# Top-k attention on one Trainium2 core: the mask by GpSimd arithmetic instead of GpSimd comparisons and a ScalarE Relu

## What is computed

```python
def attention(x):
    q, k, v = split(x @ Wqkv.T + bqkv)                 # 16 heads of 8
    q, k = layernorm(q), layernorm(k)                  # over the 8 of a head
    aw = softmax(q @ k.T / sqrt(8))                    # 256 x 256 per head
    kth = top_k(aw, 12)[..., -1:]                      # topk = int(256 * 0.05)
    aws = aw * (aw >= kth)
    o_s = (aws / (aws.sum(-1) + 1e-8)) @ v
    qf, kf = softmax(q, -1), softmax(k, -1)
    o_l = qf @ (kf.T @ v) / (qf @ kf.sum(tokens) + 1e-6)
    return (sigmoid(alpha) * o_s + (1 - sigmoid(alpha)) * o_l) @ Wproj.T + bproj

xn = layernorm(x)
y = x + attention(xn) + (xn @ W[idx] + b[idx])         # idx: one of 8, from logits and u
```

## Time and profile before

| what | value |
|---|---|
| median of 3 runs | 1330.32 us |
| lowest and highest | 1327.15 and 1330.66 us |
| span of the profiled execution | 1331.1 us, 0.8 above the median |
| instructions | 40,027 |
| mean granted TensorE clock | 0.930 of full speed |
| busy: PE, DVE, ACT, POOL | 1040.0, 1260.1, 1138.5, 1110.9 us |
| DMA, mean over the span | 62 GB/s, 82.3 MB |

### The profile page before, as it was taken

The page is one execution under the profiler, slowest core; times in us unless marked ns, Lnnn a source line. Parts: engine busy times, 40 slices in busy tenths (PEclk is TensorE's granted clock), DMA queues, the critical chain, the costliest instruction groups (busy, mean ns, idle before and its releaser), DMA issues.

```text
span 1331.1 us, 40027 instructions
## 1 busy us (share of the span) xinstructions
PE 1040.0 (78%) x8964; PEld 693.5 (52%) x8964; DVE 1260.1 (95%) x4916; ACT 1138.5 (86%) x3978; POOL 1110.9 (83%) x1458
## 2 busy tenths in 40 slices
PE   3787877778787878877888787777877788787776
PEld 1455555555455555555555455554555555555544
DVE  5799999999999999999999999999999999999995
ACT  3689998989899888989989899888989888898885
POOL 4588898979789888888879889798888888889874
PEclk9989999989899798998989989898998998989998
DMA  2222222112222122221112221112221212221210
GB/s 57 72 59 63 77 77 75 35 57 64 77 76 72 29 64 65 76 77 47 53 53 76 77 76 46 55 57 71 76 76 35 66 53 76 77 76 33 64 49 13
DMA packets 165131, 82.31 MB, mean 62 GB/s; under 512 B 7747, under 2 KB 164933, under 8 KB 164934
## 3 DMA queue, kind: packets, MB, share of 16 engines
q1 hardware_dynamic: 164934, 80.54, 20.9%
HBM read 42.77 MB, written 37.75 MB: 60 GB/s over the span
## 4 chain that ended last, share of the span: by engine, by line
DVE 57%; issue 33%; DVEq 6%; ACT 1%; POOL 1%; PE 1%; DMA 0%; SPq 0%; POOLq 0%
DVE rest L525 21%; DVE top L518 21%; DVE next L531 8%; DVEq L72 5%; DVE drop L615 2%; DVE o_sparse L574 1%; ACT e L719 1%; DVE den L566 1%; DVE k_sum L593 1%; DVE stats L582 0%; PE work_ps L910 0%; PE work_ps L911 0%; DVE x_mv L588 0%; DVE d_max L557 0%; DVE den L571 0%
## 5 line engine op out<-in xcount | busy, mean ns | idle before, releaser
L386 POOL TENSOR_SCALAR below<-e,next 128x256 bf16<-128x256 f32 x768 | 696.1, 922 | 21.5 <-DVE next L531 21.3
L719 ACT ACTIVATE e<-score_ps,drop 128x256 f32<-128x256 f32 x1024 | 472.4, 480 | 108.2 <-DVE drop L615 105.5
L838 PE MATMUL turn_ps<-ident,e 128*128 128x128 f32 x2048 | 429.9, 303 | 10.9 <-ACT kept L685 10.4
L525 DVE MATCH_REPLACE8 rest<-e 128x256 f32<-128x256 f32 x1024 | 413.3, 404 | 0.0
L531 DVE MAX8 next<-rest 128x8 f32<-128x256 f32 x1024 | 407.5, 408 | 0.0
L839 PE MATMUL turn_ps<-minus_huge,below 128*128 128x128 bf16 x2048 | 402.5, 232 | 0.0
L518 DVE MAX8 top<-score_ps 128x8 f32<-128x256 f32 x1024 | 359.4, 410 | 41.8 <-issue 21.7
L838 PEld LDWEIGHTS turn_ps<-ident,e 128*128 128x128 f32 x2048 | 312.2, 152 | 80.9 <-ACT kept L685 17.9
L685 ACT ACTIVATE kept<-turn_ps 128x512 f32<-128x512 f32 x512 | 285.1, 620 | 33.8 <-PE turn_ps L839 14.3
L839 PEld LDWEIGHTS turn_ps<-minus_huge,below 128*128 128x128 bf16 x2048 | 234.5, 115 | 0.0
L719 ACT ACTIVATION_READ_ACCUMULATOR e<-score_ps,drop 128x1 f32 x1024 | 217.1, 212 | 0.0
(11 more groups left out here) (141 smaller groups left out, 1540.6 us busy)
## 6 DMA issues: line engine op xcount, KB each, us to landing
part_slots<-part SPq DMA_DIRECT2D x128, 192.0 KB, 2.3
q_slots<-part_slots SPq DMA_DIRECT2D x64, 256.0 KB, 3.4
k_slots<-part_slots SPq DMA_DIRECT2D x64, 256.0 KB, 4.1
part_slots<-part SPq DMA_DIRECT2D x64, 128.0 KB, 1.9
x_sb<-in_L_attn_x SPq DMA_DIRECT2D x32, 128.0 KB, 3.6
x_res<-in_L_attn_x SPq DMA_DIRECT2D x32, 128.0 KB, 3.7
out_y<-out_sb SPq DMA_DIRECT2D x32, 128.0 KB, 4.2
w_ops<-in_L_ffn_W SPq DMA_DIRECT2D x1, 512.0 KB
```

Of the source, the lines that this page charges most:

```text
L386: nc.gpsimd.tensor_scalar(below[:, r, t, :], e[:, r, t, :], next8[:, r, t, TOPK - 9:TOPK - 8], None, ALU.is_lt).then_inc(s["below_pool"], 1)
L525: nc.vector.match_replace(rest[:, t, :], e8[:, (u_ - 1) % 2, t, :], e[:, (u_ - 1) % RING, t, :], REMOVED).then_inc(s["rest_ready"], 1)
L719: nc.scalar.activation(e[:, u_ % RING, t, :], score_ps[:, u_ % 2, t // 2, t % 2, :], ACT.Exp, bias=drop[:, u_ % 2, t, 0:1], accum_out=z[:, ...
L838: mm(dst, e[:, r, t, keys], ident[:], start=True, stop=False, is_transpose=True)
```

## The change

Tile 3 leaves ScalarE, and GpSimd makes the mask of all four tiles. It takes the limit times 2^40 (`limit`, 4 elements a partition), then per tile `gap` = e x (-2^40) + limit in bfloat16, and then, once per unit, `below` = max(min(gap, 2^40), 0) over all 1024 elements. GpSimd waits for all four `next` at once, for its own `limit`, and for its own four `gap`. TensorE waits for one semaphore.

```diff
-POOL_TILES = 3
...
+        limit = sb("limit", [P, 2, TILES, 1])
+        gap = sb("gap", [P, 2, TILES, N], BF16)
...
-                        r = (u_ - 2) % RING
-                        for t in range(POOL_TILES):
-                            wait_alone(pool, s["next_ready"], TILES * (g - 2) + t + 1, s["waits_passed"])
-                            nc.gpsimd.tensor_scalar(below[:, r, t, :], e[:, r, t, :],
-                                                    next8[:, r, t, TOPK - 9:TOPK - 8], None,
-                                                    ALU.is_lt).then_inc(s["below_pool"], 1)
+                        r, q = (u_ - 2) % RING, u_ % 2
+                        wait_alone(pool, s["next_ready"], TILES * (g - 1), s["waits_passed"])
+                        nc.gpsimd.tensor_scalar(limit[:, q], next8[:, r, :, TOPK - 9:TOPK - 8], HUGE, 1.0,
+                                                ALU.mult, ALU.mult).then_inc(s["limit_ready"], 1)
+                        wait_alone(pool, s["limit_ready"], g - 1, s["waits_passed"])
+                        for t in range(TILES):
+                            nc.gpsimd.tensor_scalar(gap[:, q, t, :], e[:, r, t, :], -HUGE, limit[:, q, t, :],
+                                                    ALU.mult, ALU.add).then_inc(s["gap_step"], 1)
+                        wait_alone(pool, s["gap_step"], TILES * (g - 1), s["waits_passed"])
+                        nc.gpsimd.tensor_scalar(below[:, r], gap[:, q], HUGE, 0.0,
+                                                ALU.min, ALU.max).then_inc(s["below_ready"], 1)
...
-                    if exists(it if u_ >= 2 else it - 1):
-
-                        r = (u_ - 2) % RING
-                        act.wait_ge(s["next_ready"], TILES * (g - 1))
-                        for t in range(POOL_TILES, TILES):
-
-                            nc.scalar.activation(below[:, r, t, :], e[:, r, t, :], ACT.Relu, scale=-1.0,
-                                                 bias=next8[:, r, t, TOPK - 9:TOPK - 8]).then_inc(s["below_act"], 1)
...
-                    pe.wait_ge(s["below_pool"], POOL_TILES * (g2 + 1))
-                    pe.wait_ge(s["below_act"], (TILES - POOL_TILES) * (g2 + 1))
+                    pe.wait_ge(s["below_ready"], g2 + 1)
```

More of the change, by code:

```diff
@@ L200, in build @@
             scores_ready top_ready rest_ready next_ready drop_ready e8_ready waits_passed
-            exp_done below_pool below_act turn_ready turn_copied pv_ready pv_copied
+            exp_done limit_ready gap_step below_ready turn_ready turn_copied pv_ready pv_copied
             x_stats x_mean x_rsqrt_step x_rsqrt_ready x_newton xn_ready
```

## The result

| | before | changed |
|---|---|---|
| median of the runs | 1330.49 us (4 runs) | 1401.43 us (4 runs) |
| span of the profiled execution | 1331.1 us | 1394.2 us |
| forecast | | 1342, range 1312 to 1420, slower 0.60 |

The ratio is 1.0524, with a 95% interval of 1.0502 to 1.0546: 5.2% slower. The direction was right and the time lies in the range, but I forecast 12 us more and it became 71: the size was wrong. The profiled execution of the changed kernel is the fastest of the four, 1395.92 us; the others lie at 1401.3 to 1401.8.

A forecast was written before the change was run, and what follows sets the result against it. DVE was taken to bound the kernel, with GpSimd passing it by a hair: 7.8 us over 12 pairs, 2.2 for 5 batches before the loop and 1.9 at the end, together 11.9 on 1331.1, gave 1342 us, range 1312 to 1420.

The forecast's parts named there:

- What bounds the kernel before: DVE, busy 95%, sets the pace and never waits for another engine in the steady part.
- GpSimd's queue passing DVE's: With longer units and its jump, GpSimd takes 81.0 us a pair of batches against DVE's 80.35.
- By that line `gap` is 192 + 254 x 0.82 = 400 ns: Price of GpSimd's new `gap`, by a line through the multiply-adds of the rsqrt refinement; four in a unit of 3.15 us.
- Rival E: `gap` dearer for its scalar from memory and bfloat16 output, 0.66 us each: unit 4.2, time 1570 us; chance 0.07.
- GpSimd's jump: The loop's jump back costs GpSimd 0 to 2.05 us, taken as 2.0, once in each pair of batches.
- ScalarE's part, worth 0: Taking 256 Relus, 134.0 us, off ScalarE gains nothing by itself, as it already waits for DVE.
- The cover of the new wait: Waiting for all four `next` delays GpSimd's later work 2.2 us, inside its cover; TensorE has two units, some 10 us.
- POOL at 96% or more: Sign that the forecast is right: GpSimd busy 96% or more, no longer waiting 2 us at `sq_half`.
- A: GpSimd still fits under DVE's pace, so only the end is longer: 1332 us; chance 0.24.
- B: Faster: GpSimd fits and its two-input instructions meet fewer `drop` on DVE; half of 35 us back gives 1313; chance 0.14.
- C, the hold: GpSimd's new one-input instructions hold DVE's `drop` too, 42 us in all: 1373 us; chance 0.08.
- D: Minimum and maximum on GpSimd run like the comparison, 3.1 us: unit 5.25, about 1830 us; chance 0.10.

The follow-up runs named there:

- e7: The kernel before without `drop`, ScalarE taking exp of the unshifted scores: 1269.39 us, ratio 0.9541 to the kernel before.
- e6: The changed kernel without `drop`, ScalarE taking exp of the unshifted scores: 1393.23 us, ratio 1.0472.
- e5: The changed kernel with the constant 1.0 in place of `limit` as second operand of `gap`, nothing else: 1339.65 us, ratio 1.0070.
- e2: The changed kernel without the `limit` step and its wait, `gap` made by subtract-then-multiply straight from `next`: 1958.62 us, ratio 1.4716.
- e3: The changed kernel with four of the old comparisons on GpSimd instead of `limit`, `gap` and minimum-and-maximum: 1423.96 us, ratio 1.0699.
- e4: The changed kernel with four kinds of `gap`, scalar from memory or constant, bfloat16 or float32 output, minimum-and-maximum in two halves: 1385.56 us, one run.
- e1: The changed kernel with tile 3 back on ScalarE's Relu and GpSimd's arithmetic for three tiles: 1345.67 us, ratio 1.0123.
- e9: The kernel with tile 3 back on ScalarE's Relu, run once more for its spread: 1346.81 us.

## Why the prediction was wrong in size

**What bounds the kernel before**: right. DVE sets its pace; e7 shows it (62 us less on DVE, 61.5 us less time).

**The mechanism, GpSimd's queue passing DVE's**: right for the changed kernel. e6 shows it (80 us less on DVE, 8 us less time), e5 (62 us less time for 75 ns less on each `gap`), and the batches of e2, e3 and e4, within 1% of 14.15 + 8 units. It came for a reason that my sum did not have: at the unit that I predicted, GpSimd does not pass DVE, as e5 shows. TensorE's granted clock fell from 0.930 to 0.903, which is no rival: TensorE waits for GpSimd, and GpSimd waits for the others only 5.6 us in the loop.

**The step that failed** is the term "By that line `gap` is 192 + 254 x 0.82 = 400 ns". The line came from multiply-adds with two constants, and `gap` reads one operand from memory: 480 instead of 405, by e4. From the start of the first to the end of the fourth that is 1.86 us instead of 1.55, so a unit is 3.46 (medians over the trace) and a batch of eight 2.5 us longer than in my sum. Rival E named this surcharge ("dearer for its scalar from memory and bfloat16 output"), but as a case apart at 660 ns and 0.07, and the forecast carried none of it. My own rule, 25 us for each 0.1 us of a unit, gives 1342 + 3.1 x 25 = 1420 for 3.46; the jump below takes 24 back, 1396. The profiled run has 1395.92, the median 1401.43. A forecast that sat within 0.05 us of its own threshold was near the floor of what could come, not the middle.

**GpSimd's jump**, "I take 2.0, as DVE shows 2.6": wrong, and it hid a part of the miss. At 876.74 and 918.57 us, one of which must be the jump, `sq_half` follows `k_feat` without idle. What GpSimd pays is some 0.1 us before the first `gap` of every other batch and, in 9 of the 24 batches of the loop, 0.4 to 0.9 us of waiting for DVE's `next` or ACT's cast. Charging 2.0 us to each of 12 pairs made the sum 24 us too high at this place. It also put the threshold too low: with DVE's 40.18 us a batch, (40.18 - 14.15) / 8 = 3.25 us is where a unit lets GpSimd pass, not 3.1. With my unit of 3.15 and no jump, the 7.8 us of the pairs would have gone from my sum and left 1334. So two errors of opposite sign stood in the forecast, and GpSimd passed DVE only because `gap` was dearer than I took it.

The account, from the starts of batches in the two traces, with my numbers in brackets: 0.8 us before the third `sq_half` (0), 5 batches outside the loop at 41.8 instead of 39.06, 13.7 (2.2), 12 pairs at 84.17 instead of 80.35, 45.8 (7.8), the end 2.8 (1.9). Together 63.1 (11.9). The remaining 5.5 us, by which three of the four runs are slower than the profiled one, no trace shows.

**ScalarE's part, worth 0**: right. Its 134 us of Relu went and nothing was gained by it: e3 and e5, both without the Relu, are slower than the kernel before. "ACT down by 134 us" was wrong: its busy time fell by 84, as rows overlap. Only 71 of the 134 us had no other row of ScalarE beside them.

**The cover of the new wait**: wrong in where it shows. I named `d_max` and the cast of `part`, and gave TensorE two units of cover. Both do show: DVE waits 5.0 us in all for `qkn`, and ScalarE's cast 19.5 us for `residue` (4.3 before). But the large waits are TensorE's: 78.4 us for `o_sum` (7.3 before), 70.3 for `qkn` (21.6), 28.4 for `below`. GpSimd's queue was the bound, and so its results came late at all of these places, also where I had counted on cover.

**"POOL at 96% or more"**: wrong, 86%, and it did not follow from my own sum, which has some 4.6 us a batch of GpSimd waiting for its own results. These are part of the queue and not of the busy time.

**Rivals.** A: not so, except nearly in e5. B: not so. C, the hold, happened: of the 74 `drop` that started in a minimum-and-maximum of the changed kernel, 56 had over 0.3 us of it left, and all 56 ended with it, as at 854.62 and 854.87. It hardly set the time, since the queue did: e6 puts `drop` as a whole at 8 us by the medians. D: not so, 1039 ns. E: right in kind, 480 ns and not 660, and by e4 the cause is the scalar alone. The Trainium skill ("SBUF — State Buffer", Who interferes with whom) says that a DVE instruction with two SBUF inputs contends with a GpSimd instruction that reads SBUF. The minimum-and-maximum agrees. The comparison does not, or hardly: in the kernel before, 78 `drop` started in one with over 0.3 us of it left; none ended with it, 46 took at most 0.25 us, and the longest took 0.48.

## What to carry to other kernels

When a change moves work onto an engine that is 83% busy, add up that engine's queue for one period with the waits on its own results in it, compare it with the period of the bound engine, and when the two come within the uncertainty of a price, forecast from above: the time can't fall below the other bound, but it rises with every nanosecond times the count. Take a price only from a row with the same kinds of operands and the same two operations, for one operand from memory was worth 62 us here (e5 against the changed kernel) and one other operation 557 (e2 against it, although e2 has no `limit` step). Then ask on which side of the threshold each error of the sum lies: here two of them hid one another. And look on the bound engine for an instruction that others hold back: `drop` had 36 elements and taking it out gave 4.6%, where the exp can do without the shift.

## What was unexpected of the hardware

- GpSimd's tensor-scalar on 128x256 float32: 405 ns for multiply-add with constants, 480 with one scalar from memory, 922 for a comparison with a scalar from memory, 1144 for subtract-multiply with one. Minimum-and-maximum with constants: 612 ns for 512 elements, 1039 for 1024, the same from bfloat16 and float32 (612 and 614).
- Whether a one-input GpSimd instruction holds a two-input DVE instruction (`drop`) back depends on which it is. Counted are the `drop` that started with over 0.3 us of it left. To the end of the minimum-and-maximum were held 56 of 56 in the changed kernel and 6 of 8 in e5; of the multiply-add 24 of 75 in e1 and 64 of 79 in e9, the same kernel; of the 922 ns comparison 0 of 78, and of the 1144 ns subtract-multiply of e2 0 of 131. The slower ones of these never did it.
- ScalarE's exp of 128x256 from PSUM took 480 ns with the shift read from SBUF, and 394 (e7) to 407 ns (e6) without it.
- What comes once per trip of the loop leaves DVE idle for 2.6 us, and GpSimd, with a full queue, for 0.1 us or less. That it is the jump is read from how often it comes.
